# A four-layer gated network on one core: the routed layer's weights from a tanh, the quantised layer in halves, and constant products ahead of seven handovers

## What is computed

```python
x = x + tanh(g_xattn[i]) * attention_i(layernorm(x), ctx)
x = x + tanh(g_ffn[i]) * feed_forward_i(layernorm(x))
```

```python
# feed-forward 0: both operands rounded to an 8-bit grid, scaled by their largest value
q = lambda t: round_fp8(t * (448 / max|t|)) / (448 / max|t|)
y = q(x) @ q(weight).T + bias

# feed-forward 1: 8 experts, 2 taken per token, and one shared; two iterations
logits = gelu(x @ w_r1 + b_r1) @ w_r2 + b_r2
top_p, top_i = top_k(softmax(logits), 2); top_p /= sum(top_p)
for _ in range(2):
    h = gelu([x, v] @ w1[e] + b1[e])                      # all 9 units
    alpha, beta, gate = split(h @ w2[e] + b2[e])
    alpha, beta, gate = sigmoid(alpha), softplus(beta), sigmoid(gate)
    ...                                                   # mixed over e by top_p
    x = x + sigmoid(gelu(xn @ w_h1)@w_h2) * (gelu(xn @ w_f1) @ w_f2) * iw
```

## Time and profile before

| what | value |
|---|---|
| three runs | 799.74, 800.45, 801.89 us (median 800.45) |
| the profiled execution's own time | 798.56 us |
| its span, from the first to the last instruction | 796.8 us |
| mean granted TensorE clock | 0.946 of full |
| busy: PE, DVE, ACT, POOL | 717.0, 548.8, 497.0, 170.7 us |
| attention 0, feed-forward 0, attention 1 | from 0, 126, 148 us |
| feed-forward 1, attention 2 | from 252, 413 us |
| feed-forward 2, attention 3, feed-forward 3 | from 518, 541, 702 us |

### The profile page before, as it was taken

One profiled execution on the slowest core, in us unless ns is written; L12 is line 12 of the kernel. 1 busy time (PEld: TensorE's weight loads), 2 busy tenths in 40 slices (PEclk: granted clock), 3 DMA queues, 4 the chain that ended last, 5 costly groups with the idle time before them and its releaser, 6 DMA issues. The chain is left out here.

```text
span 796.8 us, 15032 instructions
## 1 busy us (share of the span) xinstructions
PE 717.0 (90%) x5042; PEld 400.7 (50%) x5042; DVE 548.8 (69%) x1750; ACT 497.0 (62%) x1344; POOL 170.7 (21%) x162
## 2 busy tenths in 40 slices
PE   5989896899998888999789999899989999899887
PEld 3657663566664422333246666644345666544222
DVE  8599987689996377677956999755046665646533
ACT  4688882588884749599758988625676555432101
POOL 7410501460012056436634000211000000000000
PEclk9799998899998959999898999989999999999989
DMA  6694000273000000000006300000000000000000
GB/s 212 140 287 177 2 2 0 61 155 87 2 2 2 0 0 1 0 1 0 2 1 111 70 2 2 2 27 1 0 1 2 1 2 1 1 1 0 2 0 26
DMA packets 17356, 27.59 MB, mean 35 GB/s; under 512 B 1408, under 2 KB 15360, under 8 KB 16640
## 3 DMA queue, kind: packets, MB, share of 16 engines
q1 hardware_dynamic: 17280, 26.64, 12.6%
HBM read 19.03 MB, written 7.60 MB: 33 GB/s over the span
## 5 line engine op out<-in xcount | busy, mean ns | idle before, releaser
L910 ACT ACTIVATE RING<-RING,NMX 128x256 f32<-128x256 f32 x384 | 191.0, 500 | 37.7 <-DVE NMX L1885 37.5
L1885 DVE CUSTOM_DVE_ANT_0 RING<-bank,ADJM 128x256 f32<-128x256 f32 x384 | 143.9, 413 | 17.5 <-PE bank L1283 13.3
L1330 PE MATMUL bank<-W,RING 128*128 128x128 f32 x768 | 118.1, 280 | 13.5 <-ACT RING L922 12.1
L1330 PEld LDWEIGHTS bank<-W,RING 128*128 128x128 f32 x768 | 88.7, 143 | 35.5 <-ACT RING L910 25.8
L1897 DVE COPY RING<-bank 128x512 f32<-128x512 f32 x144 | 98.6, 686 | 9.2 <-PE bank L1330 8.8
L562 POOL TENSOR_TENSOR small<-small 128x2 f32<-128x2 f32 (+2 forms) x17 | 19.4, 1141 | 264.7 <-DVE small L1749 264.7
L910 ACT ACTIVATION_READ_ACCUMULATOR RING<-RING,NMX 128x1 f32 x384 | 72.6, 189 | 0.0
L824 ACT ACTIVATE RING<-bank,NMX 128x512 f32<-128x512 f32 x64 | 43.3, 683 | 42.4 <-DVE NMX L1817 22.6
L1482 PE MATMUL bank<-ARENA,W 64*128 64x512 f32 x180 | 60.8, 683 | 3.5 <-DVE ARENA L2101 2.1
L1348 PE MATMUL bank<-RING,ARENA 128*32 128x256 f32 x768 | 61.4, 394 | 0.2
L1817 DVE TENSOR_REDUCE NMX<-bank 128x1 f32<-128x512 f32 x64 | 39.4, 678 | 31.9 <-PE bank L1183 31.9
(11 more groups left out here) (270 smaller groups left out, 1313.8 us busy)
## 6 DMA issues: line engine op xcount, KB each, us to landing
scratch<-ARENA SPq DMA_DIRECT2D x18, 192.0 KB, 2.6
ARENA<-scratch SPq DMA_DIRECT2D x6, 576.0 KB, 8.8
W<-in_weights SPq DMA_DIRECT2D x1, 2564.0 KB, 22.8
scratch<-ARENA SPq DMA_DIRECT2D x18, 128.0 KB, 2.7
ARENA<-scratch SPq DMA_DIRECT2D x6, 384.0 KB, 6.1
W<-in_weights SPq DMA_DIRECT2D x2, 1024.0 KB, 14.1
W<-in_weights SPq DMA_DIRECT2D x1, 1905.5 KB, 15.2
scratch<-ARENA SPq DMA_DIRECT2D x18, 64.0 KB, 8.2
```

What stands on the lines that cost most here:

```text
L910: nc.scalar.activation(P_OF(n)[:, q * S:(q + 1) * S], S_OF(n)[:, q, :], ACT.Exp, bias=NMX[:, 2 * t + q:2 * t + q + 1], scale=-1.0, accum_o ...
L1330: mm = nc.tensor.transpose(bk[:, o:o + P], P_OF(n)[:, i:i + P], ident)
L1885: nc.vector.tensor_tensor_reduce(out=S_OF(n)[:, q, :], in0=SBANK(n)[:, q * S:(q + 1) * S], in1=ADJM[:, b, q, :], scale=-1.0, scalar=BIG, o ...
```

## The change

Three parts, together.

**Routed layer.** ACT's Exp is gone. DVE hands out FAR8, the logits less half of the second largest (`top2`), after its sixth instruction; ACT takes a Tanh of it in front of the last two Gelus of `hidden(1)`, and DVE makes the two weights as (1 + tanh) times the chosen experts, with SWI inside: two instructions of 64 columns where seven stood. `router` moves up by one product of `hidden(0)`. `weight_rows` moves up behind two of the betas, becomes transposes, and its last wait moves behind `gates(0, (NE,))`; DVE's `spread` moves in front of `first(0, (NE,))` and `second(0, (NE,))`. Four times ACT runs Gelu on one column after Softplus (`gelu_tables`), and the Tanh and Gelu behind it share one table.

**Quantised layer.** The magnitude of w8 is taken at unit 24 of attention 0 and reduced by POOL there. The bias comes behind the rounding of w8. XT is rounded in two halves, PE multiplies half by half into one bank each, and DVE adds four tiles in one instruction.

**Constant products.** `rehearse(n)` is n products of the identity and 384 columns of constants into a bank that nobody reads, 32 in all: in front of a turn and behind it 1+2 (attention 0), 4+1 (1), 3+1 (2), 5+2 (feed-forward 1), 5+2 (2), 4 in front of `keys(2)`, 2 behind the second turn of feed-forward 3.

```diff
+            pool.wait_ge(s_am, 1)
+            nc.gpsimd.partition_all_reduce(AMAXR[:, 1:2], AMAX[:, 1:2], P,
+                                           bass.bass_isa.ReduceOp.max).then_inc(s_amr, 1)
             masks(1, 0, 3)
...
             hidden(0, (0, 1, 2, 3, 4))
-            hidden(1, (0, 1, 2, 3, 4))
-            act.wait_ge(s_log, 1)
-            nc.scalar.activation(EXPL, LOG, ACT.Exp).then_inc(s_el, 1)
+            hidden(1, (0, 1, 2))
+            act.wait_ge(s_far, 1)
+            nc.scalar.activation(EXPL, FAR8, ACT.Tanh).then_inc(s_el, 1)
+            hidden(1, (3, 4))
...
             betas(1, (0, 1, 2, 3, 4, 5, 6, 7))
+            gelu_tables()
             gates(1, (0, 1, 2, 3))
...
+            def rehearse(n, bk=bank[0]):
+                for _ in range(n):
+                    nc.tensor.matmul(bk[:, 0:3 * P], ident, W[:, 0:3 * P], start=True, stop=True)
...
+                    rehearse((1, 4, 3)[a])
                     turn(XN, 0, TPB)
+                    rehearse((2, 1, 1)[a])
...
-            pe.wait_ge(s_q8, 2)
-            for t in range(NT):
-                product(rb, [(XQ[:, t * P:(t + 1) * P], W8Q[:, :])], s_fb)
+            for c in range(NC):
+                pe.wait_ge(s_q8, 2 + c)
+                bk = rb.fill(pe)
+                for i in range(4):
...
-                        mm = nc.tensor.matmul(bk[0:3 * NE, i * P:(i + 1) * P], XN[:, 4 * c + i, 0:3 * NE], ident,
-                                              start=True, stop=True)
+                        mm = nc.tensor.transpose(bk[0:3 * NE, i * P:(i + 1) * P], XN[:, 4 * c + i, 0:3 * NE], ident)
...
-                pe.wait_ge(s_eb, rb.n)
...
+                if n == 1:
+                    nc.vector.scalar_tensor_tensor(FAR8, MX2.to_broadcast([P, NT, NE]), -0.5, LOG, ALU.mult,
+                                                   ALU.add).then_inc(s_far, 1)
...
-            grid(XQ[:, :], XT[:, :], TOK, SCL[:, 0:1], T1, T2)
+            for c in range(NC):
+                grid(XQ[:, half(c)], XT[:, half(c)], 512, SCL[:, 0:1], T1[:, half(c)], T2[:, half(c)])
...
+            link(nc.vector.tensor_scalar(SEL, SEL, SWI, None, ALU.mult))
             dve.wait_ge(s_el, 2)
+            link(nc.vector.scalar_tensor_tensor(WT8, EXPL, 1.0, SEL, ALU.add, ALU.mult))
```

More of the change, by code:

```diff
@@ L1590, in _ @@
                 if c == 1:
[L1591 removed]
+                    r6.drain(pe, (0, 2, 3, 6, 7))
                     first_keys(2, 0, 2)
@@ L2005, in _ @@
             dve.wait_ge(s_qw[1], 96)
+            dve.wait_ge(s_amr, 1)
+            scale(1)
             grid(W8Q[:, :], w("w8"), D, SCL[:, 1:2], T1[:, 0:D], T2[:, 0:D])
+            for t in range(NT):
+                chain(nc.vector.scalar_tensor_tensor(X[:, t, :], w("b8"), GATE[:, 1:2], X[:, t, :],
+                                                     ALU.mult, ALU.add))
             dve.wait_ge(s_q8, 1)
+            dve.wait_ge(s_amr, 2)
+            scale(0)
             dve.wait_ge(s_ea, XT_AT[0])
-            grid(XQ[:, :], XT[:, :], TOK, SCL[:, 0:1], T1, T2)
+            for c in range(NC):
+                grid(XQ[:, half(c)], XT[:, half(c)], 512, SCL[:, 0:1], T1[:, half(c)], T2[:, half(c)])
             link(nc.vector.tensor_tensor(UNS, SCL[:, 0:1], SCL[:, 1:2], ALU.mult))
@@ L2160, in _ @@
             settle()
+            spread()
             first(0, (NE,))
             second(0, (NE,))
-            spread()
             first(0, (0, 1, 2, 3))
```

69 lines of the change are left out of this document (42 added, 27 removed).

## The result

The changed kernel took 791.6 us (median of 4 runs, 789.41 to 792.5) beside 800.45 for the kernel before (three runs, 799.74 to 801.89): ratio 0.988, 95% interval 0.986 to 0.991. Executions more than 1.5% above the fastest of their kernel, such as a fourth of the kernel before at 1013.13 us, are left out of all ratios and medians here. Run again later in six runs the changed kernel gave 789.4 us, ratio 0.986 (0.983 to 0.989). So it is faster by 9 to 11 us; 780 was predicted, with 771 to 790 as range. The profiled execution took 789.41 us with a span of 787.6, so it compares with the 796.8 of before.

A forecast was written before the change was run, and what follows sets the result against it. No engine was taken to bound the whole kernel; PE was partly slow at half clock. Routed layer -12.6, quantised -2.0, attention 0 -2.2, attention 2 -1.2, feed-forward 3 -0.6 sum to -18.6 from 798.56: 780 us, range 771 to 790.

The forecast's parts named there:

- The routed layer, forecast -12.6: Routed layer: earlier weights bring its entry forward 10.2 us and fewer table loads give 2.4; bounds -6 to -16.
- 10.2 us gained: Routed layer's entry: DVE begins `first(0, (4, 5))` at about 282.6 us instead of 292.76.
- The terms for a clock that holds: Starts of attention 0, attention 2, feed-forward 3: two thirds of the clock's gain counted, -3.4, -2.3, -1.2 before the products' delays.
- Quantised layer, forecast -2.0: Quantised layer: DVE scales and rounds during its wait for POOL, XT goes in halves; last additions end at 142.8, not 144.85.
- just in time: Quantised layer on PE: at full clock the values and four constant products end at 145.8, before the turn at 146.1.
- Table loads, forecast -2.4: Routed layer on ACT: two loads of 1.28 us saved before `hidden(3)`, less one-column Gelus; two before `refine` save nothing.
- so ACT is its bound: Routed layer from 345 us on: clock full, ACT busy 42.6 of 45 us, hence taken as bound there.
- Delay by products: Constant products overrunning PE's waits: attention 0 +1.2, attention 2 +1.1, first product of the routed layer 1.4 us later.
- Price of one: One constant product of 384 columns on PE: 0.67 us at full clock, 1.33 at half.
- The signs: Right if: 64-column activation ends near 268, Softplus 271, weights 274, attention 1's turn 146, full clock 17-28 and 255-262.
- The products only delay: Rival, whole kernel: clock falls as often as before, products add delay, total gain 8.3 us, time 790; chance 0.15.
- The routed layer gives part back: Rival, routed layer after 300 us: earlier weights only move waits, 5.9 + 1.3 of 12.6 stay, 785.4 us; chance 0.15.

The follow-up runs named there:

- e5: Changed kernel with DVE's multiplies of experts 0 and 1 put ahead of the gate's multiply that waits for ACT's first Tanh; 784.9 us, ratio 0.978.
- e6: Changed kernel with four more constant products in PE's 2.8 us wait ahead of the third weight product, queues unchanged; 790.3 us, ratio 0.986.
- e13: The changed kernel itself, unaltered, measured again in six runs; 789.4 us, ratio 0.986.
- e1: Changed kernel without any constant products and without the wait for bank 0 ahead of attention 2; 793.7 us, ratio 0.991.
- e11: Changed kernel without constant products, experts 0 and 1 multiplied before the gate on DVE, products of experts 6 and 7 before their weights on PE; 793.7 us.

## Why the prediction was wrong

Forecast from the old profile's own time: -18.6 us. Measured against it, by the marks of the table: attention 0 -1.1, quantised layer -2.6, attention 1 +2.1, routed layer -6.5, attention 2 -2.1, feed-forward 2 -0.1, the rest +1.1: -9.2.

- **The routed layer, forecast -12.6, measured -6.5.** This is the step that failed: at the start of `first(0, (4, 5))` the working has "**10.2 us gained**", and 6.2 were measured. Up to the weights the working held, counted from the layer's start: the turn behind five products, the first product 1.4 late, the router 1.8 us earlier for 2.0, the weights on PE 22.7 us after the start (272.87) for 22.3. Then I added instructions of DVE one after the other from the Tanh on. The Tanh came 1.4 us late, and the ring behind it did not run at DVE's pace: its banks come free by the very multiplies that waited, so PE and ACT stood still (2.84 and 2.44 us), and a fallen clock of 14 us, for which the sum had no term, was there as well. e5 shows it: with the multiplies ahead of the wait the mark comes 3.2 us earlier, of which filling the wait alone, for the clock, gives 1.0 (e6). Even the -6.5 has luck in it: in e13 the same kernel has 6.0 at the mark and only 0.5 at the layer's end.
- **The terms for a clock that holds.** Attention 0 and 2 gave 3.2 for 3.4, but that is luck for attention 0: it takes 110.6 to 117.4 us with products and 112.0 to 116.6 without, and in e1 its clock held from 17 to 28 without any. And there was no term for falls in new places: attention 1 (+2.1), a longer one from 743 to 751 us in feed-forward 3 (+1.1 for -0.6; the rest takes 250.9 in e5 and e6 with the same products there).
- **Quantised layer, forecast -2.0, measured -2.6, kept 0.5.** The layer's working was right in the main: 2.6 against the kernel before's own profile, and 1.5 to 2.3 against the other five executions of the old layer (19.88 to 20.62 us). What failed is that nothing stood behind it: attention 1 took it back, by its clock, in this execution by 1.1 us of products that were not "just in time" (they were in e13), and in others by the transfer.
- **Table loads, forecast -2.4, measured -0.3.** This is the second term that was mis-sized. All of the loads that it counts lie behind the mark, and from the mark to the layer's end the changed kernel takes 119.6 us for 119.9. The step behind it was "so ACT is its bound" for the stretch from 345 on: ACT's work there went from 42.6 to 37.3 us, and only 0.3 us of that reached the layer's end. With the clock taken out by the estimates above, 1 to 2 us of the term may be real; no run isolates it. By the Trainium skill, "ScalarE: Activation LUTs", section "What ACT_TABLE_LOAD costs", a switch takes 2.66 us. The trace doesn't agree here either: the load of 1.28 us starts at 268.87 and Softplus at 270.17, so 0.02 us lie between them.
- **Delay by products**: forecast 1.2, 0, 1.4, 1.1 at the four visible places, measured 2.2, 1.1, 1.4, 0.9 in this execution; of the 2.2 only 1.1 are the products', so these terms were right. Price of one: five stand from 249.33 to 252.63, 0.66 us each at full clock, for 0.67 forecast.
- **The signs.** Most that were named for being right came: the activation of 64 columns ended at 267.2, Softplus started at 270.17, `weights` at 272.87, the turn of attention 1 at 145.57, and the clock was full from 255 to 262; only that of 17 to 28 was not, for 3.4 us. None of them stood behind the step that failed, so they could not tell 780 from 790.
- **The rivals.** "The products only delay" ended nearest, 790, by luck: its picture was half clock as often as before, and it went from 86 to 47 us. By the rule of the Trainium skill weighed with it ("TensorE: Matmul & The Clock Gate", section "HAM oscillation") idle gaps as short as these cost no clock. The runs speak against that: products in just these gaps lift the mean clock, which is 0.958 at most in the executions without them and 0.961 at least in those with all of them. "The routed layer gives part back" had the right layer and the wrong place: the entry, not the ring after 300.

## To carry to other kernels

When a chain is made earlier, don't add up what follows at the pace of one engine: ask for each buffer behind it which instruction frees it and what stands in front of that instruction in its queue. Fill waits of TensorE only to their length: an overrun is on the path at once (1.4 us at the routed layer here), while a clock that is kept counts only where TensorE is the bound. Where the clock moves stages by several us from execution to execution, judge an edit by several profiled executions, by stages it doesn't touch, and by the distance between two marks within the stage: the one here repeats to 0.3 us while its stage moves by 6. And name signs that lie behind the riskiest step of a forecast, not only in front of it.

## What was not expected of the hardware

- The same program loses its clock at different places in different executions: 154.4 and 160.4 us in one stage, while a stage such as the quantised layer repeats to 0.02 us (18.35 to 18.37 in fourteen executions).
- The clock also fell with PE busy almost without a gap: from 150 to 159 us the changed kernel has PE busy for 8.86 of 9.00 us at full clock, and in the stretch from 159 to 170 above for 10.93 of 11.00 at 0.69. In e11 it fell behind a wait of 0.72 us and stayed low from 30 to 45 us with PE busy for 15.00 of 15.00. What sets it off there stays open.
- A transfer was a second limit that no view of the old profile showed as one: PE waited 0.69 us for it before, 3.02 in e5.
